# Spectral layer: GpSimd forms the sum and difference of a filter's matrices, and the second part's pair products are read from PSUM

## The chip, the cores and the metric

The kernel runs on one core of a Trainium2 chip. Its five engines are TensorE (PE, whose weight loads stand as PEld), VectorE (DVE), ScalarE (ACT), GpSimd (POOL) and SyncE (SP, which issues the transfers). The metric is the device time of one execution in microseconds, and lower is better. Over runs of this kernel a difference of 0.2% is about the smallest that can be told from none.

## The reference, cut to what matters

The program is a four-layer network on a 4 x 48 x 48 x 128 image: a state-space layer, a deformable convolution, linear attention with experts, causal attention, and last a spectral layer. Only the last one is touched. For each of 4 images it convolves 2304 tokens of 128 channels causally with 16 filters, once as they are and once with alternating signs, and multiplies each result by a 128 x 128 matrix of that filter:

```python
U_plus  = irfft(Vf * rfft(u));  U_minus = irfft(Vf * rfft(u * sgn)) * sgn
out = einsum('btkd,k,kde->bte', U_plus, s, Mpp) + einsum('btkd,k,kde->bte', U_minus, s, Mpm)
```

There are four such sets of matrices, `M_phi_plus[i]` and `M_phi_minus[i]`, for sequences of the full length, a half, a quarter and an eighth, whose results are added with weights. Because plus and minus differ by signs alone, the kernel splits tokens and taps into even and odd ones and needs, for each filter, the **sum** and the **difference** of the two matrices.

## The kernel before, in words

The function `layer3_spectral` ends with a loop over the 4 images (batches). In each, 16 filters are worked two to a loop iteration (`r` is 0 or 1, and names the buffer). A filter has `NU` = 4 **units** `u`, one for each pair of tap parity `z` and token parity `q`. So there are 4 x 16 x 4 = 256 units, numbered here within a filter from 0 to 3. The stage before it (rows of 40 slices from the 31st on) prepares the tokens; the unit loop is what fills the last quarter of the profile.

The 1152 outputs of a unit come in three parts of 384: `low_s` (first), `Uc[:, 0]` (`second`) and `Uc[:, 1]` (`third`). TensorE makes them by a scheme that shares products, in three PSUM banks: OWN, PAIR and LOW. For unit `u` its order, spread over two rounds of `filters_pair` (lines 2531 to 2555), is:

- `shared(u)` into OWN and `shared_pairs(u)` into PAIR (what parts 2 and 3 have in common; ScalarE keeps copies in `own_s` and `pair_s`);
- `first(u)` into LOW; `second(u)`, which adds to OWN and to PAIR (counted as `s_cv` 4); `third(u)` into LOW; then the mixing products `mix(u-1, 2)` of the unit before;
- `pairs(u)`, group 0, which **overwrites PAIR** with the pair products of the third part (line 2540), then `mix(u, 0)`, `shared(u+1)`, `shared_pairs(u+1)`, `mix(u, 1)`, `first(u+1)` and so on.

`mix` multiplies the finished outputs, split by ScalarE (line 2649) and GpSimd (line 2683) into two float16 halves, by the split matrices `W16`, and adds them to the totals.

VectorE (lines 2598 to 2623) takes in one order for each unit: two small adds on `low_s` (2599, 2600); `second` = OWN + pair products (2603), less the pair products shifted (2605: 256 columns; 2606: 128 columns); `third` = LOW less `own_s` (2609); `pair_2` = PAIR less `pair_s` (2611), which waits for `pairs(u)`; two adds from PSUM (2613, 2614); then `third` with `pair_2` (2618, 2620, 2621). Before the change the pair products of the second part are first copied by ScalarE from PAIR to `pair_1` (line 2661), and TensorE may overwrite PAIR when that copy is made (line 2539). 

In between, VectorE prepares the next filter's matrices in steps (`mix_step`): step 0 is the sum and difference (2568, 2569: 128 x 512), steps 1 to 4 scale and add up the four sets (2579 once, 2581 three times, each for two `z`). Step 2u stands between 2614 and 2618 of unit u, and step 2u+1 behind 2621, so that steps 0 and 1 are in unit 0, 2 and 3 in unit 1, and 4 in unit 2. ScalarE (2653) and GpSimd (2687) split the finished matrices; GpSimd's two such instructions for each filter (`mixing_low`) stand in unit 0 and in unit 3, each behind its second `low` (2683).

All orders are written out by hand; semaphores `s_ed` (VectorE's steps, 12 for each unit), `s_ea` (ScalarE's copies, 4 for each unit), `s_cv` (TensorE's groups, 6 for each unit), `s_uh`, `s_ul` and `s_ad` (matrices joined) hold them together.

Of the kernel before, what the change touches and what calls it, by code (L numbers as in the profile page):

```python
# [2126 lines left out]
def layer3_spectral(nc, w, f_scr, f_sum, out):  # L2127
# [12 lines left out]
    with ExitStack() as ctx:  # L2140
# [21 lines left out]
        kept = xr[:].rearrange("p q x -> p (q x)")[:, 0:6 * RC].rearrange("p (n x) -> p n x", n=6)  # L2162
        own_s, pair_s, pair_1, pair_2 = kept[:, 0:2, :], kept[:, 2:4, :], kept[:, 4, :], kept[:, 5, :]
# [180 lines left out]
        with nc.Fori(0, NB) as b:  # L2344
# [61 lines left out]
            with nc.Block() as block:  # L2406
# [31 lines left out]
                def _(pe):  # L2438
# [92 lines left out]
                    def filters_pair(i, last):  # L2531
                        unit = (b * KF + i * 2) * NU
                        for u in range(2 * NU):
                            r = u // NU
                            done = (unit + u) * 12 + 24
                            copied = (unit + u) * 4
                            v = (u + 1) % (2 * NU)
                            more = not (last and v == 0)
                            pe.wait_ge(s_ea, copied + 4)
                            pairs(u, FS[:, :, :, :, 1], 0, True).then_inc(s_cv, 1)  # L2540
                            mix(i, u, 0)
                            if more:
                                if v % NU == 0:
                                    pe.wait_ge(s_fl[v // NU], (b * (KF // 2) + i + (1 if v else 2)) * 64)
                                pe.wait_ge(s_ed, done + 3)
                                shared(v)
                                pe.wait_ge(s_ed, done + 7)
                                shared_pairs(v)
                            mix(i, u, 1)
                            if more:  # L2550
                                pe.wait_ge(s_ed, done + 9)
                                first(v)
                                second(v, copied + 4)
                                third(v, copied + 4)
                            mix(i, u, 2)
# [5 lines left out]
                def _(dve):  # L2561
                    def mix_step(kk, i, r, step, total):

                        if step == 0:
                            dve.wait_ge(s_ml[r], use(i, r) * 32 + 32)

                            dve.wait_ge(s_kd[r], b * (KF // 2) + i)
                            dve.tensor_tensor(Wm[:, r, 0], mab[:, r, 0], mab[:, r, 1], ALU.add).then_inc(s_ad[r], 1)
                            dve.tensor_tensor(Wm[:, r, 1], mab[:, r, 0], mab[:, r, 1], ALU.subtract).then_inc(s_ad[r], 1)
                            return  # L2570
# [18 lines left out]
                    for step in range(5):  # L2589
                        mix_step(0, 0, 0, step, base)  # L2590
                    with dve.Fori(0, KF // 2) as i:
                        unit = (b * KF + i * 2) * NU
                        for u in range(2 * NU):
# [9 lines left out]
                            dve.tensor_tensor(second, ps[:, OWN:OWN + RC], pair_1, ALU.add).then_inc(s_ed, 1)  # L2603
                            dve.wait_ge(s_ed, at + 3)
                            dve.tensor_tensor(second[:, P:], second[:, P:], pair_1[:, 0:2 * P], ALU.subtract).then_inc(s_ed, 1)
                            dve.tensor_tensor(second[:, 0:P], second[:, 0:P], pair_1[:, 2 * P:], ALU.subtract).then_inc(s_ed, 1)  # L2606
# [8 lines left out]
                            if step < 5:  # L2615
# [21 lines left out]
                def _(act):  # L2637
# [17 lines left out]
                    def filters_pair(i, last):  # L2655
                        unit = (b * KF + i * 2) * NU
                        for u in range(2 * NU):
                            r = u // NU
                            act.wait_ge(s_cv, (unit + u) * 6 + 4)
                            act.wait_ge(s_ed, (unit + u) * 12 + 17)  # L2660
                            act.activation(pair_1, ps[:, PAIR:PAIR + RC], ACT.Copy).then_inc(s_ea, 1)
# [17 lines left out]
                def _(pool):  # L2679
# [8 lines left out]

                    each = 2 * KF + 1
                    mixing_low(b * each + 1, 0, 0)  # L2690
                    with pool.Fori(0, KF // 2) as i:  # L2691
                        unit = (b * KF + i * 2) * NU
                        for u in range(2 * NU):
# [3 lines left out]
                            if u % NU == 0:  # L2697
                                mixing_low(b * each + (i * 2 + r) * 2 + 2, r, 1)
# [148 lines left out]
```

## Time and profile before

| | |
|---|---|
| median of 3 runs | 7693.79 us (7692.5 to 7694.76) |
| profiled execution | 7697.52 us, span 7695.5 us |
| busy, whole span | PE 6986.6 us (91%), PEld 5968.0 (78%), DVE 6292.1 (82%), ACT 4533.2 (59%), POOL 4643.8 (60%) |
| unit loop, all four batches | from about 5790 to 7687 us of the span |
| granted TensorE clock, mean of the execution | 0.963 |

Times are microseconds from the span's start. A row of the timeline is one instruction or a run of equal ones: start, duration, engine, line, output and inputs, count, and in brackets the idle time before it with what ended it. A row of the groups has busy time and mean duration in ns. Line numbers are those of the kernel before.

### The profile page before, as it was taken

What the parts mean: (1) busy time and instruction counts of PE and PEld (TensorE: products, weight loads), DVE (VectorE), ACT (ScalarE), POOL (GpSimd) and SP (SyncE); (2) the same over time, 40 slices, a digit from 0 to 9 for tenths busy, and PEclk for the clock granted to TensorE, in tenths of its full rate; (3) what the DMA queues carried; (4) which work ended last, traced back from release to release, by engine and by line L of the source; (5) the groups of instructions that cost most, each with busy time, mean ns of one, the idle gap of its engine ahead of it and who ended that gap; (6) DMA issues with size and microseconds to landing.
All of it is one profiled execution on the core that took longest, in us unless ns stands there. A gap on an engine that the chain in (4) does not pass through costs nothing. (4 is left out here: it accounts for less than half of the span.)

```text
span 7695.5 us, 180193 instructions
## 1 busy us (share of the span) xinstructions
PE 6986.6 (91%) x64774; PEld 5968.0 (78%) x64774; DVE 6292.1 (82%) x9149; ACT 4533.2 (59%) x9445; POOL 4643.8 (60%) x5010
## 2 busy tenths in 40 slices
PE   8999989999899998999957999888879989899898
PEld 6888768888588885888836888546648989889898
DVE  7999879998799997999945777556668878888788
ACT  5888658887588874888811333325554545545454
POOL 5888748887388882888817766222114545445454
PEclk9999999999999999999969999889989999999999
DMA  2333213332133331323347776200004434344343
GB/s 64 91 92 92 86 53 92 92 93 85 53 91 92 92 86 51 94 90 94 91 131 233 231 200 190 75 3 23 11 20 134 131 114 133 106 134 131 114 133 106
DMA packets 595164, 774.81 MB, mean 101 GB/s; under 512 B 52215, under 2 KB 528408, under 8 KB 592193
## 3 DMA queue, kind: packets, MB, share of 16 engines
q1 hardware_dynamic: 542529, 594.11, 26.0%
q0 software_dynamic: 51840, 169.91, 7.5%
q8 instruction: 523, 8.57, 0.5%
q14 instruction: 272, 2.23, 0.1%
HBM read 730.16 MB, written 33.66 MB: 99 GB/s over the span
## 5 line engine op out<-in xcount | busy, mean ns | idle before, releaser
L647 POOL TENSOR_TENSOR l_arena<-l_arena 128x768 f32<-128x768 f32 x1536 | 2596.6, 1691 | 450.3 <-DVE l_arena L579 444.2
L579 DVE TENSOR_TENSOR_SCAN l_arena<-l_arena,psum 128x772 f32<-128x772 f32 x1536 | 2662.8, 1750 | 176.7 <-PE psum L406 72.6
L500 ACT ACTIVATE l_arena<-l_arena,l_A 128x384 f32<-128x384 f32 x3072 | 1643.0, 603 | 38.2 <-DVE l_arena L579 32.8
L408 PE MATMUL psum<-l_arena 128*128 128x128 f32 x11520 | 1500.6, 280 | 45.6 <-DVE l_arena L579 41.9
L408 PEld LDWEIGHTS psum<-l_arena 128*128 128x128 f32 x11520 | 1368.6, 193 | 169.2 <-issue 145.4
L419 PE MATMUL psum<-l_ident,l_arena 128*128 128x128 f32 x9216 | 1257.6, 273 | 50.6 <-ACT l_yT L506 41.7
L419 PEld LDWEIGHTS psum<-l_ident,l_arena 128*128 128x128 f32 x9216 | 1055.2, 141 | 60.2 <-POOL l_arena L647 60.2
L2683 POOL TENSOR_TENSOR st_U<-st_Uc,st_U 128x384 f16<-128x384 f32 x512 | 470.7, 919 | 839.0 <-ACT st_U L2649 839.0
L1211 POOL DMA_INDIRECT l_G<-neighbours,l_idx x648 | 622.3, 960 | 391.6 <-issue 189.9
L490 ACT ACTIVATE l_arena<-l_arena,l_BT 128x256 f32<-128x256 f32 x1728 | 746.8, 496 | 7.5
L2500 PE MATMUL psum<-st_U,st_W 128*128 128x128 f16 (+3 forms) x6144 | 523.4, 226 | 44.6 <-POOL st_U L2683 35.2
L2649 ACT ACTIVATE st_U<-st_Uc 128x384 f16<-128x384 f32 x512 | 266.4, 520 | 477.0 <-DVE st_Uc L2606 392.5
L2475 PE MATMUL psum<-st_FS,st_xt 128*128 128x128 f16 x6912 | 518.2, 219 | 0.6 <-DMA st_FS<-filter_sums 0.6
L556 DVE TENSOR_TENSOR l_arena<-psum,l_BT 128x384 f32<-128x384 f32 x960 | 509.3, 531 | 0.0
L406 PEld LDWEIGHTS psum<-l_ident,l_arena 128*128 128x128 f32 x3456 | 380.5, 140 | 143.8 <-issue 141.3
L406 PE MATMUL psum<-l_ident,l_arena 128*128 128x128 f32 x3456 | 487.0, 277 | 2.8 <-DVE l_arena L579 2.8
L1054 DVE TENSOR_TENSOR l_G<-l_G,psum 128x1536 f32<-128x1536 f32 (+1 forms) x144 | 366.3, 2547 | 111.0 <-DMA l_G<-neighbours,l_idx 110.6
L2500 PEld LDWEIGHTS psum<-st_U,st_W 128*128 128x128 f16 x6144 | 401.6, 98 | 70.0 <-POOL st_U L2683 48.0
L2465 PE MATMUL psum<-st_F,st_xt 128*128 128x128 f16 x4608 | 427.2, 219 | 0.0
L2475 PEld LDWEIGHTS psum<-st_FS,st_xt 128*128 128x128 f16 x6912 | 420.7, 97 | 0.9 <-DMA st_FS<-filter_sums 0.8
L1259 PE MATMUL psum<-l_ident,l_G 128*128 128x128 f32 x2592 | 319.3, 283 | 68.2 <-DVE l_G L1054 40.4
L1259 PEld LDWEIGHTS psum<-l_ident,l_G 128*128 128x128 f32 x2592 | 303.6, 147 | 91.0 <-DVE l_G L1054 46.7
(469 smaller groups left out, 11981.1 us busy)
## 6 DMA issues: line engine op xcount, KB each, us to landing
l_arena<-c_rows SPq DMA_DIRECT2D x1536, 192.0 KB, 3.0
st_FS<-filter_sums SPq DMA_DIRECT2D x128, 1155.0 KB, 9.1
st_F<-filter_parts SPq DMA_DIRECT2D x128, 320.5 KB, 6.8
neighbours<-l_xt SPq DMA_DIRECT2D x256, 72.0 KB
st_mab<-in_st_mp SPq DMA_DIRECT2D x68, 256.0 KB, 9.3
st_mab<-in_st_mm SPq DMA_DIRECT2D x68, 256.0 KB, 6.6
l_G<-neighbours,l_idx POOLq DMA_INDIRECT x648, 3.7
l_arena<-in_x SPq DMA_DIRECT2D x4, 1152.0 KB, 5.2
```

The source lines that it names most:

```text
L406: mm = pe.transpose(ps[:, o:o + P], xT[:, rank[s] % 2, t, h * P:(h + 1) * P], ident[:])
L408: mm = pe.matmul(ps[:, o:o + P], dtuT[:, g % 2, t, h * P:(h + 1) * P], diagB[:, rank[s] % 3, t, :], start=True, stop=True)
L419: mm = pe.matmul(y_ps[:, t, h * P:(h + 1) * P], hC[:, s % NHC, h, t * P:(t + 1) * P], ident[:], start=(n == 0 and h == 0 and t % 2 == 0), ...
L490: ins = act.activation(xT[:, i % 2, t, :], dtuT[:, g % 2, t, :], ACT.Copy, scale=BT[:, g % 2, t, n:n + 1])
L500: act.activation(decay[:, s % NDC, half(h)], dtv[:, g % 2, h, :], ACT.Exp, scale=A[:, g // NRC, h, n:n + 1]).then_inc(s_exp, 1)
L556: dve.tensor_tensor(diagB[:, i % 3], ident_ps.unsqueeze(1).broadcast_to([P, LB, P]), BT[:, g % 2, :, n:n + 1].broadcast_to([P, LB, P]), AL ...
L579: dve.tensor_tensor_scan(hbuf[:, n, run], decay[:, s % NDC, run], x2_ps[s % 2][:, run], 0.0, ALU.mult, ALU.add).then_inc(s_scan, 1)
L647: pool.tensor_tensor(hC[:, s % NHC], halves(hbuf[:, s % NS, :]), Cs[:, s % NCS, :].unsqueeze(1).broadcast_to([P, 2, RC]), ALU.mult).then_i ...
L1211: pool.indirect_dma_start(out=G[:, g, 4 * k:4 * k + 4, :].rearrange("p q c -> p (q c)"), out_offset=None, in_=tables[b], in_offset=bass.In ...
L1259: mm = pe.matmul(bank(i % 2, P * a, P * (a + 1)), G[:, g, 4 * k + q, :], ident[:], start=(q == 0), stop=(q == 3), is_transpose=True, skip_ ...
L2475: mm = pe.matmul(ps[:, at + i * P:at + (i + 1) * P], xt[:, xpart, x0 + LB - 1 - i, :], FS[:, r, fpart, z, three, shift + i * P:shift + (i ...
L2500: mm = pe.matmul(ps[:, o:o + hi - lo], W16[:, r, wpart, z, m, :], U16[:, c, upart, lo - c * RC:hi - c * RC], start=False, stop=False, skip ...
```

## The change

The copy `pair_1` goes. ScalarE instead copies OWN into `second`, at the same place in its order and without the wait it had. VectorE then adds the pair products to `second` straight from PAIR, and makes the two subtractions from PAIR as well. TensorE may overwrite PAIR only when these are done (`s_ed`, done + 5). The sum and difference (step 0) move from VectorE to GpSimd, as `join`, into unit 0 behind its second `low`; the `mixing_low` that stood there moves to unit 1. The buffer `kept` is one piece shorter.

```diff
-                            pe.wait_ge(s_ea, copied + 4)
+                            pe.wait_ge(s_ed, done + 5)
                             pairs(u, FS[:, :, :, :, 1], 0, True).then_inc(s_cv, 1)
...
-                        if step == 0:
-                            dve.wait_ge(s_ml[r], use(i, r) * 32 + 32)
-
-                            dve.wait_ge(s_kd[r], b * (KF // 2) + i)
-                            dve.tensor_tensor(Wm[:, r, 0], mab[:, r, 0], mab[:, r, 1], ALU.add).then_inc(s_ad[r], 1)
-                            dve.tensor_tensor(Wm[:, r, 1], mab[:, r, 0], mab[:, r, 1], ALU.subtract).then_inc(s_ad[r], 1)
-                            return
...
-                    for step in range(5):
+                    for step in range(1, 5):
                         mix_step(0, 0, 0, step, base)
...
-                            dve.tensor_tensor(second, ps[:, OWN:OWN + RC], pair_1, ALU.add).then_inc(s_ed, 1)
+                            pair_ps = ps[:, PAIR:PAIR + RC]
+                            dve.tensor_tensor(second, second, pair_ps, ALU.add).then_inc(s_ed, 1)
                             dve.wait_ge(s_ed, at + 3)
-                            dve.tensor_tensor(second[:, P:], second[:, P:], pair_1[:, 0:2 * P], ALU.subtract).then_inc(s_ed, 1)
-                            dve.tensor_tensor(second[:, 0:P], second[:, 0:P], pair_1[:, 2 * P:], ALU.subtract).then_inc(s_ed, 1)
+                            dve.tensor_tensor(second[:, P:], second[:, P:], pair_ps[:, 0:2 * P], ALU.subtract).then_inc(s_ed, 1)
+                            dve.tensor_tensor(second[:, 0:P], second[:, 0:P], pair_ps[:, 2 * P:], ALU.subtract).then_inc(s_ed, 1)
...
-                            if step < 5:
+                            if 1 <= step < 5:
                                 mix_step(i * 2 + r + 1, i + r, 1 - r, step, base + (i * 2 + r + 1) * 8)
...
                             act.wait_ge(s_cv, (unit + u) * 6 + 4)
-                            act.wait_ge(s_ed, (unit + u) * 12 + 17)
-                            act.activation(pair_1, ps[:, PAIR:PAIR + RC], ACT.Copy).then_inc(s_ea, 1)
+                            act.activation(Uc[:, 0, :], ps[:, OWN:OWN + RC], ACT.Copy).then_inc(s_ea, 1)
...
+                    def join(i, r):
+                        pool.wait_ge(s_ml[r], use(i, r) * 32 + 32)
+                        pool.wait_ge(s_kd[r], b * (KF // 2) + i)
+                        pool.tensor_tensor(Wm[:, r, 0], mab[:, r, 0], mab[:, r, 1], ALU.add).then_inc(s_ad[r], 1)
+                        pool.tensor_tensor(Wm[:, r, 1], mab[:, r, 0], mab[:, r, 1], ALU.subtract).then_inc(s_ad[r], 1)
+
                     each = 2 * KF + 1
+                    join(0, 0)
                     mixing_low(b * each + 1, 0, 0)
...
                             if u % NU == 0:
+                                join(i + r, 1 - r)
+                            if u % NU == 1:
                                 mixing_low(b * each + (i * 2 + r) * 2 + 2, r, 1)
```

## Rows read from the trace of the kernel before

**Rows 1.** Busy time by engine over one filter of the unit loop.
```profile
7359.00:7386.30 27.30, 26.08 (x435) 25.06 (x434) 24.53 (x59) 14.61 (x31) 13.96 (x15) 1.00 0.45 129
```

**Rows 2.** Timeline of VectorE, units 0 to 3 of one filter, and the next unit 0's end.
```profile
7361.65 0.28 DVE L2621 TENSOR_TENSOR st_Uc<-st_Uc,st_xr 128x128 f32<-128x128 f32 x1
...
7362.45 0.28 DVE L2600 TENSOR_TENSOR st_low_s<-st_low_s 128x128 f32<-128x128 f32 x1
7362.91 0.56 DVE L2603 TENSOR_TENSOR st_Uc<-psum,st_xr 128x384 f32<-128x384 f32 x1 [0.17 <-ACT st_xr L2661]
7363.50 1.16 DVE L2605 TENSOR_TENSOR st_Uc<-st_Uc,st_xr 128x256 f32<-128x256 f32 x1
...
7367.87 0.61 DVE L2581 SCALAR_TENSOR_TENSOR st_Wm<-st_Wm,st_mweight 128x128 f32<-128x128 f32 x2
...
7376.06 0.56 DVE L2603 TENSOR_TENSOR st_Uc<-psum,st_xr 128x384 f32<-128x384 f32 x1 [0.50 <-ACT st_xr L2661]
...
7377.64 0.28 DVE L2606 TENSOR_TENSOR st_Uc<-st_Uc,st_xr 128x128 f32<-128x128 f32 x1
...
7378.31 0.54 DVE L2611 TENSOR_TENSOR st_xr<-psum,st_xr 128x384 f32<-128x384 f32 x1
...
7378.97 0.27 DVE L2614 TENSOR_TENSOR st_Uc<-st_Uc,psum 128x128 f32<-128x128 f32 x1
7379.27 0.60 DVE L2618 TENSOR_TENSOR st_Uc<-st_Uc,st_xr 128x384 f32<-128x384 f32 x1
7379.91 1.27 DVE L2620 TENSOR_TENSOR st_Uc<-st_Uc,st_xr 128x256 f32<-128x256 f32 x1
7381.10 0.28 DVE L2621 TENSOR_TENSOR st_Uc<-st_Uc,st_xr 128x128 f32<-128x128 f32 x1
...
7382.60 0.56 DVE L2603 TENSOR_TENSOR st_Uc<-psum,st_xr 128x384 f32<-128x384 f32 x1 [0.49 <-ACT st_xr L2661]
...
7390.22 0.56 DVE L2603 TENSOR_TENSOR st_Uc<-psum,st_xr 128x384 f32<-128x384 f32 x1 [0.17 <-ACT st_xr L2661]
```

**Rows 3.** Timeline of TensorE in unit 3: `pairs(u)`, then `shared_pairs(u+1)`.
```profile
7377.07 0.55 PEld L2485 LDWEIGHTS psum<-st_FS,st_xt 128*128 128x128 f16 x9
...
7378.90 0.51 PEld L2485 LDWEIGHTS psum<-st_F,st_xt 128*128 128x128 f16 x9 [0.26 <-DVE st_xr L2611]
```

**Rows 4.** Timeline of ScalarE, end of unit 0 and unit 3.
```profile
7361.97 0.52 ACT L2649 ACTIVATE st_U<-st_Uc 128x384 f16<-128x384 f32 x1 [1.17 <-DVE st_Uc L2621]
7362.40 0.47 ACT L2661 ACTIVATE st_xr<-psum 128x384 f32<-128x384 f32 x1
...
7379.63 0.49 ACT L2643 ACTIVATE st_xr<-psum 128x384 f32<-128x384 f32 x1 [0.20 <-PE psum L2485]
```

**Rows 5.** Timeline of GpSimd, end of unit 0 and unit 3.
```profile
7362.57 0.94 POOL L2683 TENSOR_TENSOR st_U<-st_Uc,st_U 128x384 f16<-128x384 f32 x1 [2.32 <-ACT st_U L2649]
7363.47 0.91 POOL L2683 TENSOR_TENSOR st_U<-st_low_s,st_U 128x384 f16<-128x384 f32 x1
...
7378.55 0.91 POOL L2683 TENSOR_TENSOR st_U<-st_Uc,st_U 128x384 f16<-128x384 f32 x1 [1.12 <-ACT st_U L2649]
7379.42 1.48 POOL L2687 TENSOR_TENSOR st_W<-st_Wm,st_W 128x512 f16<-128x512 f32 x1
```

**Rows 6.** Groups by line, span 5600 to 7695: busy time, mean ns.
```profile
L2605 DVE TENSOR_TENSOR st_Uc<-st_Uc,st_xr 128x256 f32<-128x256 f32 x256 | 277.8, 1085 | 8.9
...
L2620 DVE TENSOR_TENSOR st_Uc<-st_Uc,st_xr 128x256 f32<-128x256 f32 x256 | 162.4, 634 | 8.8
...
L2613 DVE TENSOR_TENSOR st_Uc<-st_Uc,psum 128x128 f32<-128x128 f32 x256 | 69.2, 270 | 0.0
```

**Rows 7.** Single lines of GpSimd: count, durations in ns (least/median/most).
```profile
L2687 POOL TENSOR_TENSOR st_W<-st_Wm,st_W x132: 1157/1480/1612, 5791.5 to 7679.8; 128x512 f16<-128x512 f32 x132
...
L2363 POOL TENSOR_TENSOR st_mab<-st_xr x8: 988/1007/1017, 5771.8 to 7215.8; 128x384 f32<-128x384 f32 x8
...
L647 POOL TENSOR_TENSOR l_arena<-l_arena x1536: 1662/1687/1762, 94.2 to 3857.1; 128x768 f32<-128x768 f32 x192
```

More of the change, by code:

```diff
@@ L2161, in layer3_spectral @@
         Uc, low_s = sb("Uc", [P, 2, RC]), sb("low_s", [P, BANK])
-        kept = xr[:].rearrange("p q x -> p (q x)")[:, 0:6 * RC].rearrange("p (n x) -> p n x", n=6)
-        own_s, pair_s, pair_1, pair_2 = kept[:, 0:2, :], kept[:, 2:4, :], kept[:, 4, :], kept[:, 5, :]
+        kept = xr[:].rearrange("p q x -> p (q x)")[:, 0:5 * RC].rearrange("p (n x) -> p n x", n=5)
+        own_s, pair_s, pair_2 = kept[:, 0:2, :], kept[:, 2:4, :], kept[:, 4, :]
         nought = sb("nought", [P, BANK], BF16)
```

## Prediction, made before the result was known

> **What bounds the kernel now.** I read three views: busy time over one filter, for the engine near its limit; the timeline of each engine through units 0 to 3, for what each waits on; the groups by line, for whether the pattern holds all 256 times.
>
> One filter takes 27.30 us at full clock, PE busy for 26.08 of them, DVE 24.53, ACT 14.61, POOL 13.96 [rows 1]. From one L2603 to the next is 7382.60 - 7376.06 = 6.54 us in unit 3, and 7390.22 - 7382.60 = 7.62 in unit 0, which holds L2568 and L2569; units 1 and 2 span 7376.06 - 7362.91 = 13.15 [rows 2]. In unit 3 PE stands still only before `shared_pairs`, for 0.26 us, released by L2611 [rows 3]. So PE has about 6.54 - 0.26 = 6.28 us of work in a unit; the filter's floor is 25.1, and the most that can be won is 2.2 us for each of 64 filters, 140 us. The loop that sets the rest runs PE, ACT's copy, DVE's adds, PE; in unit 0 DVE itself is late.
>
> One thing in these rows matters most. L2605 takes 1085 ns on average for 256 columns, L2620, of the same shape, 634 [rows 6]; by the 0.54 of L2611 (384 columns) and the 0.27 of L2614 (128) an unheld one should take about 0.41 [rows 2]. L2605 starts at 7363.50 while L2683 on POOL runs from 7363.47 to 7364.38, and ends 0.28 us after that; L2620 at 7379.91 meets L2687 (to 7380.90) and ends 0.28 behind it, too [rows 2, 5]. So a DVE add with both inputs in SBUF and a GpSimd add shut each other out, and the one that starts first, even by 0.03 us, finishes first. An add with one input in PSUM is not held: L2603 at 7362.91 takes its usual 0.56 with L2683 (7362.57 to 7363.51) beside it all the way [rows 2, 5]. The Trainium skill, "SBUF — State Buffer", "Who interferes with whom", states this: a VectorE instruction with two SBUF inputs contends with a GpSimd one that reads SBUF, and the second blocks fully. By that rule L2605 must wait, and the trace agrees, with a mean of 1.09 us. The same rule speaks against `join`, which is costed below.
>
> **Part 1: second part from PSUM, and its wait.** Let T be the start of L2603. ACT's copy is of the same size and follows the same `s_cv` 4, so T keeps its place behind PE. L2603 keeps its length. L2605 starts 0.59 later [rows 2]; with PSUM as one input I take its unheld pace, 0.34 until L2606 starts: L2611 with 384 columns and an add of 128 take 0.66 together to L2614, that is some 0.47 and 0.20, and 256 columns lie half way (bounds: 0.20, and today's 0.99, from 7376.65 to 7377.64). L2606 then runs T+0.94 to T+1.21; today T+1.58 to T+1.86 [rows 2]. DVE's own work falls by 0.65 us a unit, but DVE is not what units 2 and 3 wait for: it stands 0.50 before L2603 already.
>
> The new wait: PE is ready for `pairs(u)` at 7377.07, T+1.01 [rows 2, 3]; PAIR is free at T+1.21+0.05 = T+1.26. PE stands 0.25 us there; behind it are `mix(u,0)`, `shared` and everything of the next unit. `s_cv` 6 then reaches DVE 0.73 after the group's start (7378.90 to 7379.63, ACT's copy behind the same kind of group [rows 3, 4]): L2611 at T+1.99 instead of T+2.25, ends T+2.53, while PE arrives at `shared_pairs` at T+1.26+1.54 = T+2.80. So the old wait of 0.26 goes and a new one of 0.25 takes its place: units 2 and 3 run 6.28 + 0.25 = 6.5 us (6.49 below, with hundredths) against 6.54: **-0.05 each**.
>
> **Part 2: `join` on POOL, unit 0.** DVE loses L2568 and L2569. On POOL each of the two costs, alone, 1.25 us: 384 columns take 1.007, 768 take 1.687, in line 1.23, and L2687 with 512 takes 1.157 at least with a float16 output, which is the quicker kind (bounds 1.01 and 1.69) [rows 7]. POOL has 13.3 us idle in the filter; only the lock costs. The second `low` starts 0.63 after L2606's end, T+1.84, and the next instruction 0.87 later [rows 2, 5]: the sum holds POOL from T+2.71 to 3.96. DVE wants L2618 at T+2.96 (L2611 at 1.99, L2614 +0.66, +0.30): held, ends 3.96+0.40 = 4.36. The difference was waiting, ends 4.36+1.11 = 5.47 (L2687 ended 1.03 behind L2618's end, 0.13 less than alone). L2620 ends 5.47+0.28 = 5.75; L2621 starts 0.20 behind the lock and ends 5.95. From L2621's end E the chain today is ACT E+0.04, its next copy +0.43, L2603 +0.51: 7361.93 to 7362.91, **E+0.98** [rows 2, 4]. So unit 0 lasts 6.93 against 7.62: **-0.69**. PE's `mix(u,2)` waits for the third `low` about 0.2, ahead of the longer wait for `pairs`, free.
>
> **Part 3: `mixing_low` in unit 1.** It holds POOL from T+2.71 to 3.87. DVE wants its mixing step at 2.65+0.20 = 2.85, is 0.14 late, and is held; L2618 follows about 0.33 behind the lock, 4.20; L2620 4.78; L2621 5.12, E = 5.41. Then two L2581 (0.61 together, 0.344 each, so 0.53 to the next [rows 2]): L2599 at 5.86, L2600 at 6.07. ACT's high part starts E+0.04, and POOL's third `low` 0.60 later (7361.97 to 7362.57 [rows 4, 5]), at 6.05: behind L2599's start, 0.02 ahead of L2600's. Today DVE is 0.12 ahead there (7362.45 against 7362.57) and passes. If POOL takes it, `low` ends 6.93, L2600 7.07, and L2603 starts at T+7.00 instead of 6.49. A lead of 0.03 sufficed for POOL at 7363.47, so I take POOL first: unit 1 lasts 7.00 against 6.61 (13.15 less a 6.54 for unit 2): **+0.39**. The other `mixing_low`, in unit 3, now starts ahead of L2618, which ends 4.27; E = 4.93, hidden under PE. ACT's missing wait was always met. The moved `mixing_low` is needed only in unit 2. SP's load of the matrices waits for `join` of two filters earlier: free. `join` ahead of the loop costs about 1 us more on POOL, under 12 us of PE's first products: nothing.
>
> **Sum.** 6.93+7.00+6.49+6.49 = 26.91 against 27.30 or 27.31: -0.41 by 64 = -26 us. The last unit of each batch ends 0.4 earlier: -1.6. In the profiled execution 7697.5 - 28 = 7669.5; the median of the runs lies 3.7 lower, so **7666 us**, 0.45 (own range 7650 to 7680).
>
> **Rivals.**
> (a) DVE passes first in unit 1, 0.22. L2600 is then through before `low` starts and nothing holds L2603. For: the two starts lie 0.02 us apart in my sum, and each has errors of 0.05. Unit 1 is 6.5; 26.40, -0.91 by 64, less 1.6: **7633**.
> (b) The new wait outgrows the old, 0.10, slower. If L2605 is still held by POOL with an input in PSUM, PAIR is free at T+1.26+0.64 = T+1.90, PE waits 0.89 before `pairs`, and all units take at least 7.13: 28.5, +1.2 by 64: **7771**. It decides from a release at T+1.57, where four units make 27.3. Against: the flat 270 of L2613 over 256 [rows 6].
> (c) `join` is dearer, 0.10: at 1.55 each, toward the 1.69 bound and L2687's held 1.6, unit 0 is 7.53; 27.51: **7705**, no change.
> (d) PSUM inputs cost more to start, 0.05. I would need 0.13 more over two adds; each unit grows by it; 27.43: **7700**. Against: 0.270 from PSUM, 0.28 from SBUF for 128 columns [rows 2, 6]. The Trainium skill, "VectorE: DVE Perf Modes", "The TRN2 errata", has a fixed 120 cycles from PSUM against 58 from SBUF, which would be this case; by that rule the trace doesn't agree.
> (e) `join` holds DVE hardly at all, 0.08. Then unit 0 is 6.5 and unit 1 too, 25.96, **7608**. Against: L2620's 1.27 beside L2687.
>
> **Range and chances.** Low end between (e) and (a), 7614; high end past (d), 7702: this leaves out (b), most of (e), part of (c). 0.2% is 15 us: faster is below 7678, slower above 7709. Faster: 0.43 of the forecast's 0.45, (a), (e): 0.73. Same: 0.02, (c) less 0.02, (d): 0.15. Slower: (b) and the rest of (c): 0.12.
>
> **What would show it.** The first subtraction near 0.41 us in all 256 (1.06: (b)). PE's idle before `pairs` about 0.25, released by the second subtraction, and none before `shared_pairs`. GpSimd's two new instructions at 1.25 and 1.5 with the hold. L2618 at 1.3 to 1.4 in unit 0. L2600 at 1.0 in unit 1: POOL first; 0.28: (a). From L2603 to L2603 6.93, 7.00, 6.49, 6.49. I am wrong if units 2 and 3 exceed 6.6, which no lock of mine explains, or if unit 0 exceeds 7.2.

## Result, and the profile after

| | before | after |
|---|---|---|
| median of the runs | 7693.15 us (7688.24 to 7694.76) | 7611.68 us (7607.35 to 7613.47) |
| profiled execution | 7697.52 us, span 7695.5 | 7613.4 us, span 7611.5 |
| granted TensorE clock, mean | 0.963 | 0.964 |

The ratio is 0.9892 (95% interval 0.988 to 0.9905): 81.5 us faster, where 28 were forecast, and below the low end of the range, 7614. Everything below divides the 84 us between the two profiled executions.

One filter of the last image, the same view as [rows 1]. Columns: the window, its length, busy time of PE, PEld, DVE, ACT, POOL (with instruction counts), granted clock, DMA share, GB/s.
```profile
7274.00:7300.16 26.16, 25.79 (x436) 25.05 (x434) 22.20 (x56) 14.57 (x31) 16.08 (x16) 1.00 0.48 138
```
A filter takes 26.16 us instead of 27.30. PE's busy time hardly moves (25.8 for 26.1); DVE's falls by 2.3 and POOL's rises by 2.1. So what went in the loop is waiting, not TensorE's work.

VectorE over the end of unit 3, all of unit 0 and unit 1, and the start of unit 2, answering [rows 2]. L2597, L2599 and L2600 are now the three operations on `second`, L2592 and L2593 the adds on `low_s`, L2605 `pair_2`, L2612 to L2615 the last three, L2574 a mixing step.
```profile
7278.69 0.55 DVE L2597 TENSOR_TENSOR st_Uc<-st_Uc,psum 128x384 f32<-128x384 f32 x1 [0.42 <-ACT st_Uc L2654]
7279.28 0.42 DVE L2599 TENSOR_TENSOR st_Uc<-st_Uc,psum 128x256 f32<-128x256 f32 x1
...
7280.68 0.56 DVE L2605 TENSOR_TENSOR st_xr<-psum,st_xr 128x384 f32<-128x384 f32 x1 [0.31 <-PE psum L2485]
...
7285.09 0.55 DVE L2597 TENSOR_TENSOR st_Uc<-st_Uc,psum 128x384 f32<-128x384 f32 x1 [0.42 <-ACT st_Uc L2654]
...
7288.06 1.44 DVE L2612 TENSOR_TENSOR st_Uc<-st_Uc,st_xr 128x384 f32<-128x384 f32 x1
7289.53 1.38 DVE L2614 TENSOR_TENSOR st_Uc<-st_Uc,st_xr 128x256 f32<-128x256 f32 x1
7290.83 0.28 DVE L2615 TENSOR_TENSOR st_Uc<-st_Uc,st_xr 128x128 f32<-128x128 f32 x1
...
7292.08 0.56 DVE L2597 TENSOR_TENSOR st_Uc<-st_Uc,psum 128x384 f32<-128x384 f32 x1 [0.17 <-ACT st_Uc L2654]
...
7294.93 1.44 DVE L2574 SCALAR_TENSOR_TENSOR st_Wm<-st_Wm,st_mweight 128x128 f32<-128x128 f32 x2
7296.29 0.55 DVE L2612 TENSOR_TENSOR st_Uc<-st_Uc,st_xr 128x384 f32<-128x384 f32 x1
...
7297.94 0.29 DVE L2592 TENSOR_TENSOR st_low_s<-st_low_s 128x128 f32<-128x128 f32 x1
7298.14 0.29 DVE L2593 TENSOR_TENSOR st_low_s<-st_low_s 128x128 f32<-128x128 f32 x1
7298.47 0.56 DVE L2597 TENSOR_TENSOR st_Uc<-st_Uc,psum 128x384 f32<-128x384 f32 x1
```
Three things are to be seen. The first subtraction takes 0.42, no longer 1.16: nothing holds it (420 to 423 ns in all 256). From L2597 to L2597 it is 6.40, 6.99 (unit 0, with 1.44 and 1.38 where GpSimd's `join` holds VectorE) and **6.39 in unit 1, where 7.00 was forecast**. And the second `low_s` add in unit 1 takes 0.29.

GpSimd beside it, answering [rows 5].
```profile
7287.82 1.27 POOL L2685 TENSOR_TENSOR st_Wm<-st_mab 128x512 f32<-128x512 f32 x1
7289.04 1.58 POOL L2686 TENSOR_TENSOR st_Wm<-st_mab 128x512 f32<-128x512 f32 x1
...
7294.80 1.16 POOL L2680 TENSOR_TENSOR st_W<-st_Wm,st_W 128x512 f16<-128x512 f32 x1
7298.13 1.07 POOL L2676 TENSOR_TENSOR st_U<-st_Uc,st_U 128x384 f16<-128x384 f32 x1 [2.17 <-ACT st_U L2643]
7299.16 0.91 POOL L2676 TENSOR_TENSOR st_U<-st_low_s,st_U 128x384 f16<-128x384 f32 x1
```
L2676 is recorded as starting at 7298.13, 0.01 ahead of L2593, and takes 1.07 instead of 0.91: here GpSimd was the one that waited.

TensorE's weight loads: `pairs(u)` and, 1.5 us behind, `shared_pairs(u+1)`, answering [rows 3]; the first of `third(u+1)`; and ScalarE's copy for that unit.
```profile
7279.28 0.54 PEld L2500 LDWEIGHTS psum<-st_U,st_W 128*128 128x128 f16 x9
7279.95 0.51 PEld L2485 LDWEIGHTS psum<-st_FS,st_xt 128*128 128x128 f16 x9
...
7281.44 0.55 PEld L2485 LDWEIGHTS psum<-st_F,st_xt 128*128 128x128 f16 x9
...
7284.32 0.21 PEld L2465 LDWEIGHTS psum<-st_F,st_xt 128*128 128x128 f16 x3
```
```profile
7284.57 0.49 ACT L2654 ACTIVATE st_Uc<-psum 128x384 f32<-128x384 f32 x1
```
PE is released for `pairs` at 7279.95, T+1.26, and doesn't stop before `shared_pairs`, both as forecast. ScalarE's copy starts 0.25 us behind the first weight load of `third`. In the kernel before that distance is 0.34:
```profile
7375.20 0.21 PEld L2465 LDWEIGHTS psum<-st_F,st_xt 128*128 128x128 f16 x3
...
7375.54 0.49 ACT L2661 ACTIVATE st_xr<-psum 128x384 f32<-128x384 f32 x1
```

The groups of VectorE and GpSimd over the unit loop, answering [rows 6, 7] (busy, mean ns).
```profile
L2599 DVE TENSOR_TENSOR st_Uc<-st_Uc,psum 128x256 f32<-128x256 f32 x256 | 107.7, 421 | 8.8
...
L2593 DVE TENSOR_TENSOR st_low_s<-st_low_s 128x128 f32<-128x128 f32 x256 | 72.3, 283 | 0.0
```
```profile
L2680 POOL TENSOR_TENSOR st_W<-st_Wm,st_W 128x512 f16<-128x512 f32 x131 | 151.6, 1157 | 9.8 <-ACT st_W L2647 9.8
L2686 POOL TENSOR_TENSOR st_Wm<-st_mab 128x512 f32<-128x512 f32 x67 | 105.5, 1575 | 0.0
L2685 POOL TENSOR_TENSOR st_Wm<-st_mab 128x512 f32<-128x512 f32 x67 | 85.2, 1271 | 22.9 <-DMA st_mab<-in_st_mm 22.9
```

The last place is between two images. From the last L2603 (now L2597) of one image to the first of the next is 50.5 us on average before and 47.1 after (three such stretches each; 50.35, 50.54, 50.70 and 49.14, 46.26, 46.03). The last one, first of before, then of after; columns as above:
```profile
7195.30:7246.00 50.70, 32.16 (x266) 28.76 (x263) 22.97 (x51) 13.64 (x29) 14.59 (x18) 0.76 0.44 142
```
```profile
7134.70:7180.70 46.00, 29.61 (x265) 27.99 (x263) 20.98 (x50) 13.17 (x28) 16.51 (x20) 0.81 0.46 150
```
The same number of PE instructions (266 and 265 in the records), done in 2.5 us less at a mean granted clock of 0.81 instead of 0.76.

The account of the 84 us, from the starts of all 256 additions: the four images' unit loops 430.3 us each before and 412.2 after, 72.3 together; the three stretches between, 10.2; the start of the loop 1.3; the end 0.2. Of the 10.2, 1.1 is still the end of an image: its last mixing product ends 7.36 us behind its last addition before and 6.99 after (means of three). By unit (medians):

| from addition to addition, us | unit 0 | unit 1 | unit 2 | unit 3 | image | stretches between |
|---|---|---|---|---|---|---|
| before | 7.62 | 6.62 | 6.54 | 6.53 | 430.3 | 50.4, 50.5, 50.7 |
| forecast | 6.93 | 7.00 | 6.49 | 6.49 | | unchanged |
| after | 6.99 | 6.38 | 6.39 | 6.41 | 412.2 | 49.1, 46.3, 46.0 |

Three questions follow. Why are units 1 to 3 each 0.1 shorter than the sum of waits says? Who takes the port in unit 1 (what VectorE and GpSimd shut each other out of), and by what lead? And why did the stretch between images, of which the change touches little but one wait, shrink?

### The profile page after: what moved, and what is told of

It reads as the page before. It is cut to its first block and busy times, and to the rows that moved or that the text cites. A ratio compares the mean times of both kernels' runs of the same rounds, so it can differ in the third digit from the quotient of the medians.

```text
span 7611.5 us, 179937 instructions
## 1 busy us (share of the span) xinstructions
PE 6957.3 (91%) x64774; PEld 5963.9 (78%) x64774; DVE 6138.4 (81%) x9013; ACT 4529.1 (60%) x9445; POOL 4786.6 (63%) x5146
## 5 line engine op out<-in xcount | busy, mean ns | idle before, releaser
L2676 POOL TENSOR_TENSOR st_U<-st_Uc,st_U 128x384 f16<-128x384 f32 x512 | 480.1, 938 | 644.5 <-ACT st_U L2643 644.5
```

What stands on the lines that cost most here:

```text
L2676: pool.tensor_tensor(U16[:, c, 1, :], src, U16[:, c, 0, :], ALU.subtract).then_inc(s_ul, 1)
```

## The experiments

The unit lengths of each run are medians over 64 units. ScalarE's old wait is the one on `s_ed`, which is always met long before.

**A wait that is met, put back.** The kernel after, with ScalarE's old wait behind the one on TensorE.
```diff
                             act.wait_ge(s_cv, (unit + u) * 6 + 4)
+                            act.wait_ge(s_ed, (unit + u) * 12 + 17)
                             act.activation(Uc[:, 0, :], ps[:, OWN:OWN + RC], ACT.Copy).then_inc(s_ea, 1)
```


> The kernel after with one line put back: ScalarE's wait for s_ed, long met, between its wait for s_cv 4 and the copy of OWN. In the kernel after, the copy starts 0.25 us behind the start of third(u) on TensorE, in the kernel before 0.34. Theory 1: a second wait behind the one that ends last costs about 0.09 us each time, although it is always met, and this is what units 1 to 3 won beyond the forecast. Then units 1 to 3 go from 6.39 to 6.47-6.49 us, 192 of them, and the kernel takes about +17 us, 7628. Rival: the copy starts earlier because of something else (another bank, no reader on DVE at that time): nothing changes, 7612.

Measured: 7638.36 us, ratio 0.9926 (0.9913 to 0.9939); units 7.00, 6.46, 6.47, 6.49; image 416.1; between 50.4, 49.9, 50.0. Units 1 to 3 each lose 0.08. ScalarE's copy again starts late behind the first weight load of `third`, 0.33 us, in unit 2 of one filter:
```profile
7293.20 0.21 PEld L2465 LDWEIGHTS psum<-st_F,st_xt 128*128 128x128 f16 x3
```
```profile
7293.53 0.49 ACT L2655 ACTIVATE st_Uc<-psum 128x384 f32<-128x384 f32 x1
```
The time is 10 us above what was expected, and nearly all of that stands between the images (8.8 us more than in the kernel after), which no theory had named. Unit 0 didn't change; there ScalarE reaches the copy late in any case, behind its high part of the unit before.

**The same two waits, exchanged, in the kernel before.** The one that ends last now stands last.
```diff
-                            act.wait_ge(s_cv, (unit + u) * 6 + 4)
                             act.wait_ge(s_ed, (unit + u) * 12 + 17)
+                            act.wait_ge(s_cv, (unit + u) * 6 + 4)
```


> The kernel before with ScalarE's two waits ahead of the copy of PAIR in the other order: first the one that is long met (s_ed), then s_cv 4, which is then the last one ahead of the copy. No work is changed. Theory 1: the copy, L2603 and L2611 all come 0.09 us earlier and PE's wait before shared_pairs shrinks from 0.26 to 0.17: units 1 to 3 go from 6.53-6.62 to 6.45-6.53, -0.09 x 192 = -17 us, 7676; unit 0, which DVE sets, keeps its 7.62. Rival (the order does not matter): 7693.

Measured: 7678.06 us, ratio 0.9979 (0.997 to 0.9987); units 7.62, 6.54, 6.46, 6.46; image 426.8; between 50.5, 51.0, 50.7. The same 0.08 is won in the kernel before by order alone, 15 us in all, and nothing between the images.

**The wait ahead, in the kernel after.** As the first experiment, with the order of the second.
```diff
+                            act.wait_ge(s_ed, (unit + u) * 12 + 17)
                             act.wait_ge(s_cv, (unit + u) * 6 + 4)
                             act.activation(Uc[:, 0, :], ps[:, OWN:OWN + RC], ACT.Copy).then_inc(s_ea, 1)
```


> The kernel after with the long-met wait for s_ed put back ahead of the wait for s_cv 4 instead of behind it. It tells two costs of that wait apart. Theory: behind the late wait it costs 0.08 us a unit; ahead of it nothing, as ScalarE passes it while it is still waiting for TensorE. So units 1 to 3 stay at 6.39, and of the +25 us with the wait behind, some 16 go. Second theory: the stretch between two batches (last L2603-like add to the first of the next batch) is 50 us in the kernels that have this wait and 46 in those without, because ScalarE's program is longer: then the stretches stay near 50 and the kernel takes about +8 us against 7612, 7620. Rival to the second: stretches 46, 7612.

Measured: 7619.06 us, ratio 0.9907 (0.989 to 0.9923); units 6.99, 6.38, 6.39, 6.41 and image 412.2, as in the kernel after; between 49.5, 50.1, 49.1, near the 50.4 to 50.7 of the kernel before. The medians of this kernel and of the kernel after are too close to be told apart; it is the traces that differ. So one unneeded wait has two prices: 0.08 a unit by its place, and 2 to 3 us a stretch by being there at all.

**The kernel before without that wait.** This is safe: before the group that `s_cv` 4 counts, TensorE has itself waited for more of VectorE's steps.
```diff
                             act.wait_ge(s_cv, (unit + u) * 6 + 4)
-                            act.wait_ge(s_ed, (unit + u) * 12 + 17)
```


> The kernel before without ScalarE's long-met wait for s_ed ahead of the copy of PAIR (the order is held through TensorE's waits). Nothing else changes. Theory: units 1 to 3 as with the two waits swapped, 6.54, 6.46, 6.46 (-0.08 x 192 = -16 us), and the stretches between batches fall from 50.5 to 46-47 us as in all kernels that lack this wait (-4 x 3 = -12 us): about 7665. Rival: the shorter stretches come from part 1's other edits, and the kernel ends where the swapped one did, 7677.

Measured: 7670.28 us, ratio 0.9967 (0.9954 to 0.9979); units 7.62, 6.54, 6.45, 6.45; image 426.7; between 47.1, 47.7, 47.4. Both prices are saved, without anything else of the change: 14 us in the images, some 9 between. In the pages, the queue that carries instructions differs with it: first the kernel before, then this one (packets, MB).
```profile
q14 instruction: 272, 2.23, 0.1%
```
```profile
q14 instruction: 256, 2.10, 0.1%
```
And ScalarE's first work for the last image, before, then after; then for the second image in the run with the wait ahead, and in this one:
```profile
7212.44 2.31 ACT L2399 ACTIVATE st_xp<-st_xn 128x768 f32 x3 [11.20 <-issue]
```
```profile
7146.45 2.31 ACT L2399 ACTIVATE st_xp<-st_xn 128x768 f32 x3 [6.52 <-PEq L2406]
```
```profile
6229.94 2.31 ACT L2399 ACTIVATE st_xp<-st_xn 128x768 f32 x3 [11.19 <-issue]
```
```profile
6240.45 2.31 ACT L2399 ACTIVATE st_xp<-st_xn 128x768 f32 x3 [6.69 <-PEq L2406]
```
With 272 or 273 packets ScalarE stands 11.0 to 11.2 us before this copy, and in "issue", which is no wait that the profile shows; with 256 or 257 it stands 6.5 to 6.7, in a wait for another engine. That holds in all 42 such stretches of the fourteen kernels: 15 of the first kind, 27 of the second.

What follows from it can be read on TensorE. ScalarE's copy feeds VectorE and GpSimd, and these make what TensorE transposes next (L2393). Between the second image and the third, first of before, then of after:
```profile
6739.53 0.54 PE L2393 MATMUL psum<-st_ident,st_mab 128*128 128x128 f32 x3 [0.50 <-POOL st_mab L2371]
6741.59 0.87 PE L2393 MATMUL psum<-st_ident,st_Wm 128*128 128x128 f32 x6 [1.51 <-POOL st_Wm L2367]
```
```profile
6697.78 2.11 PE L2393 MATMUL psum<-st_ident,st_mab 128*128 128x128 f32 x15
6699.72 1.15 PE L2393 MATMUL psum<-st_ident,st_Wm 128*128 128x128 f32 x9
```
Such stops between the transposes add up to 1.9 to 3.4 us in each of the 15 stretches, and there is none in the 27. From the first transpose to the first product behind them (L2448) it is 13.6 to 14.4 us in the 15 and 10.4 to 10.9 in the 27. So most of the difference is shown: ScalarE starts late, GpSimd with it, and TensorE waits for GpSimd.

The whole stretch is 49.1 to 51.1 us long in the first kind and 45.9 to 47.9 in the second, but for four of 48.9 to 50.7: the first of the kernel after, the first of each of the two kernels with a small operation added below, and the second of the last kernel. In these four the transposes are as quick as in the rest of their kind (10.7 to 10.9); behind the products TensorE waits 1.9 to 2.8 us for the transfer of `filter_sums`, and then takes 5.0 to 6.2 us to the image's first addition instead of 3.6, with a mean granted clock over the stretch of 0.76 to 0.79 and not 0.81 or 0.82. Why ScalarE stands in "issue" is open; that it waits for its own code is only inferred.

**Part 1 alone.** The kernel before with the pair products read from PSUM; `join` stays on VectorE and `mixing_low` in unit 0.
```diff
-                            pe.wait_ge(s_ea, copied + 4)
+                            pe.wait_ge(s_ed, done + 5)
...
-                            dve.tensor_tensor(second, ps[:, OWN:OWN + RC], pair_1, ALU.add).then_inc(s_ed, 1)
+                            dve.tensor_tensor(second, second, pair_ps, ALU.add).then_inc(s_ed, 1)
...
-                            act.wait_ge(s_ed, (unit + u) * 12 + 17)
-                            act.activation(pair_1, ps[:, PAIR:PAIR + RC], ACT.Copy).then_inc(s_ea, 1)
+                            act.activation(Uc[:, 0, :], ps[:, OWN:OWN + RC], ACT.Copy).then_inc(s_ea, 1)
```


> The kernel before with part 1 of the change alone (second part from PSUM; join and mixing_low stay where they were). By the lock rule as the trace after bears it out: units 1 to 3 at 6.39, 6.39, 6.41 as after; unit 0: mixing_low on POOL from T+2.71 holds L2568 until T+3.87, it ends at 4.41, L2569 at 5.02, L2621 at 6.15, next L2603 0.97 later: 7.12 against 7.62 before and 6.99 after. Sum 26.3, -1.0 x 64 = -64 us: 7629, or some 10 less if the shorter stretch between batches comes with this part. Rival: if the join is what made most of the gain, about 7665.

Measured: 7622.11 us, ratio 0.9908 (0.9893 to 0.9922); units 7.13, 6.39, 6.39, 6.41; image 414.5; between 46.2, 46.3, 45.9. This part brings 71 of the 81.5 us, the removed wait with both its prices among them.

**Part 2 alone.** The kernel before with `join` on GpSimd and `mixing_low` in unit 1.
```diff
+                    def join(i, r):
...
+                                join(i + r, 1 - r)
+                            if u % NU == 1:
                                 mixing_low(b * each + (i * 2 + r) * 2 + 2, r, 1)
```


> The kernel before with part 2 and 3 alone (join on GpSimd, mixing_low in unit 1; pair_1 and ScalarE's two waits as before). By the lock rule: low of the second part still runs T+2.49 to 3.40, so join holds POOL from 3.4 on and meets L2620 and L2621 instead of L2618: unit 0 about 7.4 (7.62 before); in unit 1 mixing_low falls between the two L2581 and L2600 comes late: about 7.1 (6.62 before); units 2 and 3 stay at 6.54. Sum 27.6 against 27.31, +17 us: 7710. Rival: taking 1.07 us of unit 0 off VectorE is a gain of its own, up to -1.07 x 64 = -68: 7625.

Measured: 7710.1 us, ratio 1.0019 (1.001 to 1.0028); units 7.49, 6.91, 6.63, 6.53; image 434.2. Alone the move costs 15 us (0.19%, about the least that can be told; the four images of its trace are 15.6 us longer, too): unit 0 wins 0.13, unit 1 loses 0.29 and unit 2 0.09. Unit 1 loses nothing when part 1 is there. So the two parts don't add up: alone they make +71 and -15, together 81.5, and the move pays only behind part 1, where it takes the image from 414.5 to 412.2.

**Who takes the port: VectorE made a little later.** The kernel after, with one tiny operation of VectorE (128 x 1) behind the last mixing step of unit 1, and so ahead of the two `low_s` adds.
```diff
                             if step + 1 < 5:
                                 mix_step(i * 2 + r + 1, i + r, 1 - r, step + 1, base + (i * 2 + r + 1) * 8)
+                            if u % NU == 1:
+                                dve.memset(t1b[:], 0.0)
```


> The kernel after with one tiny VectorE instruction (a memset of one column of a spare tile) ahead of the two adds on low_s at the end of unit 1. In the kernel after, GpSimd's third low starts 0.19 us behind the first of these adds and 0.01 ahead of the second, and yet the second passes it. The memset moves both adds by some 0.05 to 0.15 us. Theory A (the one that starts first takes the port; 0.01 was too little): GpSimd now gets in ahead of the second add, which ends some 0.8 us late, and unit 1 goes from 6.38 to 6.9-7.0: +35 us, about 7647. Theory B (a VectorE add that stands directly behind another keeps the port): unit 1 stays under 6.45, 7612 to 7616.

Measured: 7647.67 us, ratio 0.9941 (0.9924 to 0.9957); unit 1 takes 7.03 in 58 of its 64 turns and 6.38 in the other 6. A second such operation, `dve.memset(top_inv[:], 0.0)`, behind the first:

> As the run with one memset, with two of them (about 0.1 to 0.3 us): GpSimd's low starts ahead of both adds or between them. Theory A: the first add is held or the second is: unit 1 at 6.9 to 7.1, 7645 to 7655. Theory B: if the first add still starts ahead of low, unit 1 stays near 6.4 to 6.5; if it starts behind it, it is held as well, and the same 6.9 to 7.1 follows.

Measured: 7652.14 us, ratio 0.9951 (0.9934 to 0.9967); unit 1 takes 7.03 in all 64. One turn, VectorE and then GpSimd:
```profile
7326.82 0.29 DVE L2592 TENSOR_TENSOR st_low_s<-st_low_s 128x128 f32<-128x128 f32 x1
...
7327.02 1.03 DVE L2593 TENSOR_TENSOR st_low_s<-st_low_s 128x128 f32<-128x128 f32 x1
7327.98 0.54 DVE L2597 TENSOR_TENSOR st_Uc<-st_Uc,psum 128x384 f32<-128x384 f32 x1
```
```profile
7326.99 0.91 POOL L2679 TENSOR_TENSOR st_U<-st_Uc,st_U 128x384 f16<-128x384 f32 x1 [2.18 <-ACT st_U L2646]
```
The same two instructions as at 7298.13 and 7298.14, with GpSimd 0.03 ahead instead of 0.01, and the roles are exchanged: 1.03 on VectorE, 0.91 on GpSimd. By the single starts of all turns, in ns, GpSimd's lead over the second add was 6 to 15 in the kernel after and VectorE passed each time; with one operation added it was 19 or 20 in the six turns in which VectorE passed, and 19 to 26 in the 58 in which GpSimd did; with two, 27 to 33, GpSimd always. By recorded starts the change of hands is at a lead of 0.02 us. The held adds stand directly behind another add as well, so that place alone doesn't keep the port for VectorE.

**`join` cut in two.** To win unit 0 back: the difference stays in unit 0, the sum moves to unit 2 of the filter before, so that each holds VectorE once.
```diff
                             if u % NU == 0:
-                                join(i + r, 1 - r)
+                                join(i + r, 1 - r, 1)
...
+                            if u % NU == 2 and not (last and r == 1):
+                                join(i + 1, r, 0)
```


> The kernel after with join cut in two: the difference stays in unit 0, the sum is made by GpSimd in unit 2 of the filter before, where it has no other matrix work (the last iteration of its loop is written out, as on the other engines, since it has no sum to make in its last filter). So each unit has one long GpSimd instruction behind its second low. Theory (the lock): a unit with one of them hides it, as units 1 and 3 do with mixing_low (6.38, 6.41), and unit 0's 6.99 is two of them holding L2618 and L2620 in turn. Then all units take 6.38 to 6.45, 25.6 a filter against 26.16: -0.55 x 64 = -35 us, 7577. Rival: unit 0 is long because its mixing step waits for join, or because GpSimd itself is late: then it stays near 6.9 and unit 2 may grow, 7605 to 7620.

Measured: 7600.64 us, ratio 0.9882 (0.9866 to 0.9899); units 6.40, 6.39, 6.83, 6.41. Unit 0 came down by 0.59, as expected; unit 2 went up by 0.44, which wasn't, and varied from 6.39 to 7.41. GpSimd's sum there waited for its matrices:
```profile
7292.73 1.61 POOL L2686 TENSOR_TENSOR st_Wm<-st_mab 128x512 f32<-128x512 f32 x1 [0.99 <-DMA st_mab<-in_st_mm]
```
So in the next kernel SyncE issues them ahead of a filter's taps, the next filter's pair first:
```diff
-                    with sp.Fori(0, KF // 2) as i:
+                    load_matrices(1, 0, 1)
+                    with sp.Fori(0, KF // 2 - 1) as i:
...
+                        load_matrices(k2, i + 1, 0)
+                        load_filter(k1, i, 1)
+                        load_matrices(k3, i + 1, 1)
+                        load_filter(k2, i + 1, 0)
```


> The kernel with join cut in two, and SyncE issues a filter's matrices ahead of the taps of the filter before instead of behind them. With join cut in two, unit 0 came down to 6.40 but unit 2 rose to 6.83, since its sum waited 1.0 us for the matrices' transfer and so met L2614-like adds late. Theory: with the matrices there, the sum holds VectorE's mixing step in unit 2 as mixing_low does in unit 1, but step 4 has one wait more (0.25 us): unit 2 at about 6.6, 7601 - 0.2 x 64 = 7587. Rival: the load was not what counted and unit 2 stays at 6.83, 7601.

Measured: 7600.04 us, ratio 0.9878 (0.9863 to 0.9893); unit 2 still 6.80, now in 60 of its 64 turns within 0.02. GpSimd's sum no longer waits, and the unit is as long: the late transfer explains the spread, not the length. What is left there is mixing step 4, which now meets the sum and stands ahead of the last additions, so the next experiment moves it behind unit 2's last subtraction.
```diff
-                            if 1 <= step < 5:
+                            if 1 <= step < 4:
                                 mix_step(i * 2 + r + 1, i + r, 1 - r, step, base + (i * 2 + r + 1) * 8)
...
-                            if step + 1 < 5:
-                                mix_step(i * 2 + r + 1, i + r, 1 - r, step + 1, base + (i * 2 + r + 1) * 8)
+                            if step + 1 < 6:
+                                mix_step(i * 2 + r + 1, i + r, 1 - r, min(step + 1, 4), base + (i * 2 + r + 1) * 8)
```


> As the run with early loads, with VectorE's mixing step 4 behind the last add of unit 2 instead of in its middle. Theory: unit 2 then has in its middle only the held add, like unit 3, and the step falls into VectorE's idle time: all four units at 6.39 to 6.41, 25.6 a filter, and the kernel at about 7572. The risk is the 0.02 us at which GpSimd's third low gets in ahead of the second add on low_s: by my sum this add starts some 0.05 ahead of low; if it goes the other way unit 2 is 7.0 and the kernel 7611.

Measured: 7606.02 us, ratio 0.9883 (0.9868 to 0.9898); unit 2 takes 6.96. Units 1 and 2 of this run show both outcomes of the race in one kernel, VectorE first, then GpSimd:
```profile
7290.48 0.28 DVE L2600 TENSOR_TENSOR st_low_s<-st_low_s 128x128 f32<-128x128 f32 x1
...
7296.62 0.29 DVE L2599 TENSOR_TENSOR st_low_s<-st_low_s 128x128 f32<-128x128 f32 x1 [0.24 <-DVE st_Wm L2581]
7296.83 1.00 DVE L2600 TENSOR_TENSOR st_low_s<-st_low_s 128x128 f32<-128x128 f32 x1
```
```profile
7290.47 1.07 POOL L2683 TENSOR_TENSOR st_U<-st_Uc,st_U 128x384 f16<-128x384 f32 x1 [2.17 <-ACT st_U L2650]
...
7296.73 0.96 POOL L2683 TENSOR_TENSOR st_U<-st_Uc,st_U 128x384 f16<-128x384 f32 x1 [1.95 <-ACT st_U L2650]
```
A lead of 0.01 loses and one of 0.10 wins. The row of L2599 also names the mending: VectorE stands 0.24 waiting for its own step 4, only to announce that the matrices are done. The last kernel makes that announcement behind the adds.
```diff
-                        if m == 3:
+                        if m == 3 and announce:
                             dve.wait_ge(s_mm, total + 8)
                             dve.sem_inc(s_wm[r], 1)
...
                             dve.tensor_tensor(low_s[:, 2 * P:RC], low_s[:, 2 * P:RC], edge_s, ALU.subtract).then_inc(s_ed, 1)
+                            if u % NU == 3:
+                                dve.wait_ge(s_mm, base + (i * 2 + r + 1) * 8 + 8)
+                                dve.sem_inc(s_wm[1 - r], 1)
```


> e10_step_later, but the announcement of the finished matrices (a wait of VectorE for its own mixing step 4, and the count for ScalarE and GpSimd behind it) moves from the end of unit 2 behind the two low_s adds of unit 3. In e10_step_later VectorE stood 0.24 us in that wait ahead of the low_s adds; GpSimd's third `low` began 0.10 ahead of the second add, which was held to 1.00 us, and unit 2 took 6.96. Theory: the port goes to the one that starts first. Without the wait the adds start 0.24 earlier, the second some 0.14 ahead of GpSimd, more than the 0.02 that decides; it passes in 0.28 and unit 2 falls to 6.4 like the others. Batch from first to last add 411.2 - 64/4... = 16 x 0.56 = 9.0 less, 402; four batches 36 us less than e10_step_later: 7570. Rival: GpSimd's start follows VectorE's last add closely and the second add is held all the same, or the hold moves to unit 3: 7606.

Measured: **7574.09 us** (7572.54 to 7577.44), ratio 0.9844 (0.9831 to 0.9858), some 37 us less than the kernel after by the two ratios; units 6.40, 6.39, 6.39, 6.41, image 402.8, between 46.4, 49.6, 46.1. The same instructions in the same unit, the second add now 0.23 ahead (0.14 expected), VectorE, then GpSimd:
```profile
7295.31 0.28 DVE L2599 TENSOR_TENSOR st_low_s<-st_low_s 128x128 f32<-128x128 f32 x1
7295.51 0.28 DVE L2600 TENSOR_TENSOR st_low_s<-st_low_s 128x128 f32<-128x128 f32 x1
```
```profile
7295.74 0.92 POOL L2686 TENSOR_TENSOR st_U<-st_Uc,st_U 128x384 f16<-128x384 f32 x1 [1.95 <-ACT st_U L2653]
```
A filter now takes 25.57 us, and the records show PE busy for all of it (the ends of matmuls are modelled). The weight loads, PEld, are the stricter measure: they are busy for 25.05, and in each unit they still stand 0.13 us (by the median; 0.14 in unit 2) before `pairs`.
```profile
7274.00:7299.57 25.57, 25.57 (x435) 25.05 (x433) 22.11 (x57) 14.55 (x31) 15.75 (x17) 1.00 0.46 141
```

## Why the prediction was wrong in size, point by point

The direction and the locks were right. Three terms were not: who takes the port in unit 1 (39 us, the step on which the forecast turned), a wait put at nothing inside the units (12 us), and the same wait between the images (9 us).

**What bounds the kernel: right.** The gain came from waits, PE's work stayed, and the rule that an addition with an input in PSUM isn't held while one with two in SBUF is, read from L2603 and L2605 [rows 2, 5], held in all 256 units: L2599 takes 420 to 423 ns.

**Part 1, the new wait for the old one: right by mechanism, too small by 0.08 to 0.1 a unit.** Release of `pairs` at T+1.26, `pair_2` at T+1.99, no stop before `shared_pairs`: each as forecast to 0.01. The stop before `pairs` is 0.13 or 0.14 by the medians of units 0, 2 and 3, not 0.25 (`mix` ends at 7279.28 + 0.54 = 7279.82); only in unit 1, behind the long unit 0, is it 0.43. The step that failed is "T keeps its place behind PE", with "ACT's missing wait was always met", costed at nothing. T came 0.09 earlier behind PE, since a wait that stands behind the one that ends last takes its own time after that end, though it is met. Units 2 and 3 are 6.39 and 6.41 instead of 6.49: 0.10 and 0.08 by 64, 12 us. The exchange in the kernel before, its removal there, and its return behind and ahead of the other wait in the kernel after tell the same 0.08. The forecast's own sum has a slip besides: 6.28 + 0.25 is 6.53, and the 6.49 carried on rests on 1.54 us from `pairs` to `shared_pairs`, where [rows 3] give 1.83 less the stop of 0.26, 1.57. With the measured stop 6.28 + 0.13 = 6.41 comes out, as measured.

**Part 2, `join` in unit 0: right.** 6.99 against 6.93. The sum starts at T+2.73 (2.71 forecast) and takes 1.27, the difference ends at T+5.53 (5.47), L2612 takes 1.44 (1.40). The error of 0.06 lies in the 1.25 an instruction, for which 1.27 stands, and in the held one.

**Part 3, `mixing_low` in unit 1: this is the step that failed.** Every start up to the race came as forecast: `mixing_low` at T+2.72 (2.71), L2612 at 4.21 (4.20), the adds at 5.86 and 6.06 (5.86, 6.07), `low` at 6.05 (6.05). The choice on top, "a lead of 0.03 sufficed for POOL, so I take POOL first" with 0.02 forecast, was wrong: the lead was 0.006 to 0.015, the border lies at 0.02, and VectorE passed in all 64 turns. That is rival (a), which had 0.22. The prediction itself gave each start an error of 0.05, so neither outcome could be had from its rows; to have named POOL or DVE would have been luck. Instead of +0.39, unit 1 won 0.24: 0.61 by 64 is 39 us, of which 0.5 by 64 = 32 are the lock, and the rest the wait above (rival (a) had 6.5, not 6.38). The Trainium skill, "SBUF — State Buffer", "Who interferes with whom", says that the order of issue, not the shape of the operation, decides who blocks. The rows agree at leads of 0.03 and 0.10; at 0.01 the one whose recorded start is the later got it. Whether a recorded start is not the issue that the page means, or not precise enough to name the first within 0.02 us, no run tells.

**What wasn't in the sum: the stretch between the images**, 9 of its 10 us. The prediction had the end of each image 0.4 earlier, and it came 0.37 earlier. The rest is again "ACT's missing wait was always met", costed at nothing: the experiment with the wait ahead and the kernel before without it separate it from all other edits. Between the images that wait is worth 8.8, 7.3 and 9.4 us in the three kernels that tell it, and the stops between the transposes show by which way it costs.

**The rest of the rivals.** (b), (d): L2599 is not held, and PSUM inputs cost no more (0.28 for 128 columns at L2600, 0.28 from SBUF before [rows 2]): out. (c), (e): `join` costs 1271 and 1575 ns and holds VectorE for both: out. The four errors, 39 + 12 + 9 less unit 0's 4, are 56 us, and 56 lie between the forecast 28 and the profiled 84.

**The range** ended at 7614, between (e) and (a), with (a) at 7633 and no spread of its own. What came is (a) with the other errors on it: 7633 less 0.11, 0.10 and 0.085 by 64 (19 us), less 9, plus 4, is 7609, and 7612 was measured. That this lies only 2 us below the range is chance: it misses the forecast, 7666, by 54.

## What to carry to other kernels

A wait that was always met wasn't free here: leave such a one out, and if it must stay, put it ahead of the wait that ends last. Where two engines share a port and a forecast puts their starts within some 0.03 us, the two outcomes are two cases of equal weight (here 0.6 us in each of 64 units); better to move one of them clear, as the last kernel does by taking 0.24 us of waiting out of VectorE's way. And after a change that shortens an engine's program, look at the stretches where the program moves on to other code as well as at the loop.

## What the runs showed of the hardware beyond what was expected

- A second, long-met wait of ScalarE costs 0.08 us behind the wait that ends last (0.34 or 0.33 against 0.25 us from PE's weight load to the copy), nothing ahead of it.
- An operation of VectorE with both inputs in SBUF that starts back to back behind another passes a GpSimd instruction whose recorded start lies up to 0.016 us earlier (all 512 turns of eight kernels with a lead of 0.005 to 0.016), and is held for its whole length (to 1.04 us instead of 0.28) when that start lies 0.027 us or more earlier. At 0.02 both occur.
- 16 packets more in the instruction queue (272 or 273 for 256 or 257) go with 4.5 us more idle time of ScalarE ahead of each image's preparation, in 15 stretches against 27 without an exception, and with 1.9 to 3.4 us in which TensorE waits between transposes. Why is open.
- Four of the 27 were long all the same (48.9 to 50.7 us), with a late transfer of `filter_sums` and a mean granted clock of 0.76 to 0.79.
- In the fastest kernel TensorE's weight loads fill 25.05 of a filter's 25.57 us, and the stops before `pairs` (0.13 us in each of four units) are the rest. The floor of 25.1 estimated from [rows 3] is near: in the unit loop hardly more than TensorE's own work is left.
